# Attention in a fused fp32 kernel: new-key products once per pair of batches, five split heads instead of four, a weight split moved a stage ahead, tiles re-addressed

## The reference, cut to what matters

```python
x = x + einsum('bct,bcd->bdt', x, W0[ids0])                  # three small residual maps,
x = x + einsum('bsi,boi->bso', x, W1[ids0])                  # each batch with weights of its own
x = x + einsum('bct,bcd->bdt', x, W2[ids1]) + bias[ids1]
# attention over a paged cache: 64 batches, 32 new rows each, 32 query heads, 8 key heads, D = 128
q, k, v = x @ Wq.T, x @ Wk.T, x @ Wv.T                       # then norm and rotation of q and k
kc = k_cache[block_table]; vc = v_cache[block_table]         # 16 pages of 32 keys: 512 cached keys
scores = einsum('bqhd,bkhd->bhqk', q, concat([kc, k])) / sqrt(D)
scores = where(valid, scores, -1e30)                         # 512 cached + 32 new keys = 544
probs = softmax(scores)
x = x + (einsum('bhqk,bkhd->bqhd', probs, concat([vc, v])) @ Wo.T)
```

## Time and profile before

| | us |
|---|---|
| median of 3 runs | 2288.32 (2285.64 to 2289.05) |
| the profiled execution | 2286.66 |
| its span | 2284.8 |

### The profile page before, as it was taken

How to read it: one execution, slowest core, us unless ns; L and a number is a source line. 1 busy time by engine, 2 the same in 40 slices (tenths; PEclk the granted TensorE clock), 3 DMA queues, 4 the chain that set the end, 5 groups by cost and what they waited for, 6 DMA issues and landing times. The chain is left out here.

```text
span 2284.8 us, 52315 instructions
## 1 busy us (share of the span) xinstructions
PE 2231.2 (98%) x16384; PEld 1935.1 (85%) x16384; DVE 1675.9 (73%) x3504; ACT 1297.7 (57%) x2643; POOL 1137.8 (50%) x1218
## 2 busy tenths in 40 slices
PE   7998999999998999999999999999999998999999
PEld 6777777777776999999999999999999997888887
DVE  7860788888887888888888888888888886422221
ACT  6732888888886555555555555555555555311111
POOL 5200354544445777777777777777777773000000
PEclk9999999999998999999999999999999999999999
DMA  6643243444347888888888888888888885543442
GB/s 263 217 107 92 86 127 114 132 134 127 116 140 244 302 303 300 299 297 300 297 290 289 292 297 299 298 301 295 302 300 292 300 298 188 188 139 105 121 129 64
DMA packets 451816, 501.70 MB, mean 220 GB/s; under 512 B 95863, under 2 KB 390775, under 8 KB 443416
## 3 DMA queue, kind: packets, MB, share of 16 engines
q1 hardware_dynamic: 414872, 366.44, 49.3%
q0 software_dynamic: 36864, 134.23, 16.6%
HBM read 408.21 MB, written 92.34 MB: 219 GB/s over the span
## 5 line engine op out<-in xcount | busy, mean ns | idle before, releaser
L1192 POOL TENSOR_TENSOR att_probs<-att_probs,att_inverse 128x512 f32<-128x512 f32 x512 | 535.9, 1047 | 255.0 <-DVE att_inverse L1402 250.7
L1300 ACT ACTIVATE att_probs<-att_probs,att_low 128x544 f32<-128x544 f32 x512 | 383.7, 749 | 472.9 <-DVE att_low L1389 472.9
L1256 PE MATMUL att_o<-att_probs_t,att_values 128*128 128x128 f32 x4096 | 541.0, 275 | 2.1 <-DMA att_values<-L_cond_v_cache,att_v_rows_of 1.8
L1256 PEld LDWEIGHTS att_o<-att_probs_t,att_values 128*128 128x128 f32 x4096 | 497.6, 192 | 2.5 <-DMA att_values<-L_cond_v_cache,att_v_rows_of 2.0
L1389 DVE CUSTOM_DVE_ANT_0 att_probs<-att_score,att_mask,att_batch_cols 128x544 f32<-128x544 f32 x512 | 400.6, 782 | 129.2 <-PE att_score L1218 84.6
L1398 DVE COPY att_probs_t<-att_turn 128x512 f32<-128x512 f32 x512 | 351.0, 686 | 1.2 <-PE att_turn L1233 1.2
L1178 POOL DMA_INDIRECT att_values<-L_cond_v_cache,att_v_rows_of x256 | 270.8, 1058 | 82.5 <-POOL att_v_rows_of L1174 50.1
L1233 PE MATMUL att_turn<-ident,att_probs 128*128 128x128 f32 x2048 | 310.1, 274 | 0.8 <-POOL att_probs L1192 0.4
L1005 POOL TENSOR_TENSOR proj_q_out<-proj_by_cos,proj_by_sin 128x512 f32<-128x512 f32 x128 | 188.6, 1474 | 216.8 <-DVE proj_by_sin L931 216.8
L1233 PEld LDWEIGHTS att_turn<-ident,att_probs 128*128 128x128 f32 x2048 | 241.9, 141 | 36.2 <-issue 8.8
L862 PE MATMUL proj_proj<-x3t_hi,proj_w_hi 128*128 128x512 f32 x640 | 254.6, 398 | 6.7 <-DVE proj_w_lo L916 6.7
(11 more groups left out here) (156 smaller groups left out, 4101.1 us busy)
## 6 DMA issues: line engine op xcount, KB each, us to landing
keys_first<-L_cond_k_cache SPq DMA_DIRECT2D x512, 128.0 KB
att_keys_raw<-L_cond_k_cache SPq DMA_DIRECT2D x512, 128.0 KB
q_t<-proj_q_out SPq DMA_DIRECT2D x32, 1024.0 KB, 5.4
o_t<-att_heads_out SPq DMA_DIRECT2D x64, 512.0 KB, 6.6
out_o_raw<-o_t SPq DMA_DIRECT2D x31, 1024.0 KB, 5.3
queries_first<-q_t SPq DMA_DIRECT2D x32, 512.0 KB
att_queries_raw<-q_t SPq DMA_DIRECT2D x32, 512.0 KB
maps_even<-L_cond_weight SPq DMA_DIRECT2D x8, 1024.0 KB, 12.3
```

The costliest lines, as they stand in the source:

```text
L1192: nc.gpsimd.tensor_tensor(probs[:, k, 0:L], probs[:, k, 0:L], inverse[:, k:k + 1].to_broadcast([P, L]), ALU.mult).then_inc(probs_ready, 1)
L1256: last = nc.tensor.matmul(o_ps[:, at:at + P], values[j][:, t, h * D:(h + 1) * D], probs_t[m % 2][:, t * P:(t + 1) * P], start=(t == 0 and ...
L1300: nc.scalar.activation(probs[:, k, :], probs[:, k, :], ACT.Exp, bias=low[k][:, 0:1], scale=-1.0, accum_out=total[k][:, 0:1]).then_inc(exp_ ...
```

## The change

Five parts.

1. *One passage for a pair.* The products with the new values of both batches, 16 products, come once, in iteration 2 of the next pair. Each of the four banks of `o_ps` now holds the outputs of four heads of 128 columns, and the outputs of a pair go out in four copies, two in iteration 2 and two in iteration 3, into one tile. `new_probs_t` has four buffers. The outputs of both batches of the last pair are stored at the end.
2. *Five split heads.* NATIVE is 3, ACT_FROM 3, DVE_FROM 4: heads 3 to 7 are split. The parts grow from 384 and 512 to 480 and 640 elements, DVE writes the mask in head 3 and parts in heads 4 to 7, 0 and 1 (before: mask in head 4, parts in heads 5 to 7 and 0 to 2).
3. *The first head's weights* are split at the end of `stage_maps_values`, into buffers placed high. SP no longer waits there for the stores of the new values; POOL does so in the next stage. The wait for the stores of the new keys moves to the end of the projection.
4. *Addresses.* `keys_first`, `queries_first` and the first output head's `o0` lie in the high region. The built program places the value weights `wvt`, `o0`, `new_probs_t` and `heads_out` 32 bytes off a multiple of 64 before, and at multiples of 64 after.
5. POOL's first gather waits for the last weighing of the batch before (`weighed[1]`), where it waited for the passage.

```diff
-            w_hi[0] = a_.sb("w_hi0", [P, M, IC, P], F32R)          # now the high buffers w_first
+        a_.sb("to_64_bytes", [P, 8])
...
+            for m in range(1 + REP):                               # stage_maps_values, DVE, at the end
+                dve.wait_ge(w_hi_ready, m + 1)
+                nc_v.tensor_tensor(w_first_lo[:, m]..., w_nat[:, m, :], f32(w_first_hi[:, m])..., ALU.subtract).then_inc(w_ready, 1)
...
+            act.wait_ge(w_nat_loaded, 32)                          # stage_maps_values, ACT
+            for m in range(1 + REP):
+                copy(w_first_hi[:, m].rearrange("p c e -> p (c e)"), w_nat[:, m, :]).then_inc(w_hi_ready, 1)
...
-            for m in range(M):                                     # stage_projection, ACT and DVE
-                split_weights(0, 0, m, True)
...
-    NATIVE = 4
-    ACT_FROM, DVE_FROM = 4, 5
+    NATIVE = 3
+    ACT_FROM, DVE_FROM = 3, 4
...
-                            pool.wait_ge(o_done, i * N + j * HK)
+                            pool.wait_ge(weighed[1], i * HK + j * (HK // 2))
...
-                at = (h % GH) * BANK + (h // GH) * P
+                at = (m % GH) * BANK + (m // GH) * P
...
-                if h == HK - 1:
-                    pe.wait_ge(new_loaded[j], back * NLD + NLD)
-                    pe.wait_ge(new_kept, back * (N // GH) + (j + 1) * (HK // GH))
-                    for g in range(HK // GH):
+                if m == N - 1:
+                    for v in range(2):
+                        pe.wait_ge(new_loaded[v], back * NLD + NLD)
+                    pe.wait_ge(new_kept, back * (N // GH) + (N // GH))
+                    for g in range(N // GH):
...
-                    if h == 2 and (n >= HK or not first):
-                        keep_o(i, n - 3)
+                    if n in (2, 3) and not first:
+                        keep_o(i, range((n - 2) * 2, (n - 1) * 2))
```

More of the change, by code:

```diff
@@ L835, in _ @@
             heads(sp, head)
+            for rc in range(RC):
+                sp.wait_ge(k_stored[rc], 16 * HK)
         @block.tensor
@@ L874, in _, with split_weights @@
         def _(act):
-            def split_weights(h, u, m, first=False):
-                if m == 0 and not first:
+            def split_weights(h, u, m):
+                if m == 0:
                     act.wait_ge(w_loaded, h * 32)
@@ L975, in head @@
                         scale_k(h, SCALE_AT[t])
-            for m in range(M):
-                split_weights(0, 0, m)
             dve.wait_ge(first_pages_loaded, 16)
@@ L1008, in _ @@
             nc.gpsimd.memset(ones[:], 1.0).then_inc(ones_ready, 1)
+            for u in range(2):
+                pool.wait_ge(v_stored[u], 16 * GB * (G // 2))
             heads(pool, head)
@@ L1064, in stage_attention @@
         inverse = a_.sb("inverse", [P, RING])
-        new_probs_t = [a_.sb(f"new_probs_t{n}", [P, P]) for n in range(2)]
-        heads_out = [a_.sb(f"heads_out{v}", [P, HK, P]) for v in range(2)]
+        a_.sb("to_64_bytes", [P, 8])
+        new_probs_t = [a_.sb(f"new_probs_t{n}", [P, P]) for n in range(N // GH)]
+        heads_out = a_.sb("heads_out", [P, 2, HK, P])
+        a_.sb("foot", [P, 128])
         wot0_hi = a_.sb("wot0_hi", [P, REP, HID], F32R)
         wot0_lo = a_.sb("wot0_lo", [P, REP, HID], F32R)
-        o0_hi = a_.sb("o0_hi", [P, REP, CB, S], F32R)
-        o0_lo = a_.sb("o0_lo", [P, REP, CB, S], F32R)
+        o0_hi, o0_lo = o_first
         wo0_raw = w_nat[:, 0:REP, :]
@@ L1141, in _ @@
                 sp.wait_ge(q_stored[n], 16 * HK * (RC // 2))
-            for rc in range(RC):
-                sp.wait_ge(k_stored[rc], 16 * HK)
             sp.wait_ge(pages_ready, 1)
@@ L1308, in new_part, with keep_o @@
                 act.wait_ge(new_turned, back * (N // GH) + (g + 1))
-                if g >= HK // GH or not first:
-                    act.wait_ge(o_done, back * N + g // (HK // GH) * HK)
-                nc.scalar.activation(new_probs_t[g % 2][:], new_ps[:, 0:P], ACT.Copy).then_inc(new_kept, 1)
-            def keep_o(i, n):
-                m = n % N
-                back = i if n >= 0 else i - 1
-                j = m // HK
-                act.wait_ge(o_done, back * N + (j + 1) * HK)
-                act.wait_ge(o_stored[j], back * 16)
-                for r in (slice(0, GH // 2), slice(GH // 2, GH)):
-                    nc.scalar.activation(heads_out[j].rearrange("d (g r) n -> d r g n", r=GH)[:, r],
-                                         o_ps.rearrange("d (r k) -> d r k", r=GH)[:, r, 0:HK // GH * P].rearrange("d r (g n) -> d r g n", n=P),
+                if g == 0 and not first:
+                    act.wait_ge(o_done, i * N)
+                nc.scalar.activation(new_probs_t[g][:], new_ps[:, 0:P], ACT.Copy).then_inc(new_kept, 1)
+            def keep_o(pairs, banks):
+                act.wait_ge(o_done, pairs * N)
+                for v in range(2):
+                    act.wait_ge(o_stored[v], pairs * 16 - 16)
+                for r in banks:
+                    nc.scalar.activation(heads_out.rearrange("d v (g r) n -> d r (v g) n", r=GH)[:, r],
+                                         o_ps[:, r * BANK:(r + 1) * BANK].rearrange("d (g n) -> d g n", n=P),
                                          ACT.Copy).then_inc(o_ready, 1)
@@ L1357, in _ @@
             new_part(PAIRS, -1)
-            keep_o(PAIRS, -1)
+            keep_o(PAIRS, range(GH))
         @block.vector
```

84 lines of the change are left out of this document (47 added, 37 removed).

## The result

The changed kernel takes 2332.5 us (median, 2330.78 to 2334.57), the kernel before 2287.08 in the same comparison: a ratio of 1.0198 with a 95% interval of 1.0181 to 1.0216. The forecast was 2296 and the range ended at 2316. The direction was right and the size was not: 45 us instead of 10.

The account below looks back on a forecast made before the run. Prediction: PE's row and POOL's chain bound attention together (both 14.76 us). From 2286.66: POOL's chain +8.7, DVE +7.8, first pair +1, end +1.5, boundary -4.2, addresses -4.8, so +10.0; forecast 2296 us, range 2262 to 2316.

Parts of the forecast that it names:

- PE's own row: Attention: larger passage +0.45, lost passage -0.82, two more split heads -0.34; PE's row alone -0.71 us a pair.
- POOL's chain keeps the second batch: Heads 10 to 14: POOL's chain stays 14.76 us against PE's 13.77, so the pair comes to +0.28, +8.7 us over 31.
- DVE's longer parts: Attention: the part before masks 8 and 0 grows by 0.24 us; taken as 0.25 a pair, +7.8 us (0 to +22).
- The first rival: Attention: PE's row is all that counts, POOL's hold dissolves, DVE keeps up: -22 us there, 2258 in all; chance 0.25.
- The sentence of the prediction on the lock: DVE and POOL's shared port: the longer part starts only when POOL is done, the whole added 0.24 us behind the lock.
- DVE costs nothing: Attention: POOL holds, but late masks fall into PE's room: 2288.9 us, no change that can be told; chance 0.17.
- DVE costs all: Attention: DVE's longer parts cost +22 us instead of +7.8, 0.72 a pair: 2311 us; chance 0.15.
- remark on late keys: Attention loop: keys loaded later, behind the outputs' store one iteration more, would also end near 2311 us.
- Edges: Between maps and projection -4.2 us (-1.5 to -6.9); addresses in output and value products -4.8 (0 to -6).
- the 1 us hoped for from the clock: Projection's start: a shorter gap may spare part of the first 4 us at 1.2 GHz: -1 us (up to 2, or none).
- First pair and end of attention: First pair needs all six parts one head earlier: +1 us (0 to +2); end has four copies and larger passage: +1.5.

Follow-up runs that it names:

- e8: Changed kernel with four split heads and POOL's copy of the row numbers one head earlier: 2270.2 us, ratio 0.9925 to the kernel before.
- e16: Changed kernel with low parts of two pages (output not the reference's), next keys' loads ahead of the stores, row numbers copied one head earlier: 2271.6 us, ratio 0.9935.
- e6: Changed kernel with DVE writing low parts of only two pages of each keys part in the loop (output not the reference's): 2301.1 us, ratio 1.0063.
- e10: Changed kernel with next keys' loads ahead of the stores and row numbers copied one head earlier: 2311.7 us, ratio 1.0106.
- e3: Changed kernel's edges, addresses and five split heads, but a passage for each batch as in the kernel before: 2320.0 us, ratio 1.0150.
- e1: Changed kernel with SP's loads of the next pair's first keys ahead of the new values' loads and outputs' stores: 2334.2 us, ratio 1.0204.
- e12: Changed kernel with low parts of two pages (output not the reference's) and next keys' loads ahead of the stores: 2294.6 us, ratio 1.0035.
- e2: Changed kernel with four split heads as before, the one passage for a pair kept: 2297.9 us, ratio 1.0047.
- e14: Changed kernel with keys' loads ahead of the stores, row numbers copied one head earlier, gathers in heads 3, 4, 6, 7: 2328.2 us, ratio 1.0187.
- e7: Changed kernel with POOL's copy of the row numbers one head earlier: 2312.6 us, ratio 1.0107.
- e11: Changed kernel with keys' loads ahead of the stores, row numbers copied one head earlier, gathers in heads 3, 5, 7, 1: 2444.0 us, ratio 1.0681.

## Why the prediction was wrong, step by step

*PE's own row*: right where it could be seen. Iteration 2 was 3.44 (forecast 3.4 to 3.5), head 3 2.11, iteration 10 without its passage 2.17. With four split heads the terms give 37.11 + 0.45 - 0.82 = 36.74, and e8 has 36.72. The 36.40 of five split heads no run reached; e16 came to 36.72.

*POOL's chain keeps the second batch*: right in mechanism. With four split heads it held 14.97 against the 14.76 worked out, the passage cost 0.51 a pair where its terms without the split heads give 0.45, and moving the copy of the row numbers released it (e8). The first rival (PE's row alone, 2258) falls.

*DVE's longer parts, taken as 0.25 a pair with 0.72 as the upper end*: this is the step that failed. Shortening them gave back 1.04 (changed to e6) and 1.25 (e10 to e16). The five split heads, parts and PE's gain together, cost 1.01 on top of the passage and 1.29 without it, where the forecast's terms give 0.08 and -0.09. The pair's growth of 1.52 instead of 0.53 is most of the 36.5 us between forecast and result: (1.52 - 0.53) x 31 = 31. The working counted the longer part once, between the copy and the next mask. It treated the chain of POOL, 11.30 from the multiplication of head 2 to that of head 6, as a constant. But that chain held gathers of 1.12, and the 1.12 itself contained a wait for DVE's part, as the earlier trace rows show once a gather's end is held against a part's end. So 96 elements more made each such gather 0.10 longer, and head 4, which had no part before, now has one: some 0.4 in POOL's chain over the gathers in a row. e3, with a passage for each batch as before, shows the whole: the chain taken as 11.30 takes 12.07 in its median pair. That delayed the multiplications that the next parts wait for, and so the masks behind them, 8 and 0 among them. The sentence of the prediction on the lock spoke of the part that waits for POOL, and left out POOL that waits for the part.

The Trainium skill, page "SBUF — State Buffer", section "Who interferes with whom", has DVE instructions with two SBUF inputs contend with GpSimd instructions that read SBUF, with whoever issues first holding the other up. That agrees with the part that waits for the multiplication. The same section infers that such an instruction does not hold up descriptor generation, since that needs the write interface. Here every one of the 144 gathers issued during such a part ended 0.85 or 0.86 after it; for these gathers the measurement decides. An indirect gather also reads its row numbers, as `bass.IndirectOffsetOnAxis(ap=v_rows_of...)` in the kernel says; whether it waited with that or with its descriptors, no run here shows.

*Rivals.* "DVE costs nothing" (2288.9) falls with e6. "DVE costs all" (2311, chance 0.15) came nearest, 21 too low, and by its number only: its 0.72 a pair, too, had no POOL waiting for a part. Its remark on late keys was right in that they came late, and wrong in that they counted: with the keys ahead the pair changes by 0.17 at most (e1, e10, e12).

*Edges*: forecast -9.0 for boundary and addresses together, measured -6.4 (-4.1 to -8.7). The gap shrank by 3.2 as forecast, but the 1 us hoped for from the clock mostly did not come: 0.54 was granted for 3.6 us, where the earlier trace rows had 0.50 for 4. The maps stage ended 3.8 sooner instead of 1.9, how much of it by the addresses was not tried alone. The output's products gained 4 ns, not 5. The projection's extra 1.6 and the 0.7 behind it were in no term.

*First pair and end of attention*: both mis-sized. From the first scores to those of the second pair it took 45.05 instead of 42.07, 3.0 more where the forecast had 1 (0 to 2). The end cost more than its 1.5: PE stood 1.44 longer (3.70 for 2.26), the larger passage took 0.45 more, as in the loop, and then came the products at the lower clock, which the sum did not have.

*Left open*: why iteration 13 carries 2.8 and the part 1.92 in the changed kernel. That part (1258.38 to 1260.30) spans a whole gather and a multiplication; that it lets both go first is read from the rows and was not tried apart. Parts as slow as this one are not a matter of length: e2 has them with 384 elements (1.59) and e12 with 320 (1.53). e8, e10 and e16, with the row numbers early, have none.

## What to carry to other kernels

Before an engine's chain is taken as a constant, hold the ends of its instructions against what runs beside them on the other engines: a duration that is 0.12 above the shortest of its kind may be a wait that grows with the change. When work is made larger on an engine that alternates with another over something they share, its price is the whole alternation, counted as often as it repeats. A product moved away takes its room with it; look for who lived in that room, and move that engine's idle wait (here 0.8 for row numbers) elsewhere in the same step.

## What the runs showed of the hardware that was not expected

- An indirect gather issued while DVE writes a low part (two inputs in SBUF, the engines' on-chip memory) ends 0.85 to 0.86 after the part: 1.05 with 320 elements (e16), 1.12 with 384 (before), 1.22 with 480 (changed), 1.39 with 640 (e14). Where it meets no part it takes 0.98 to 1.01, and issued just ahead of a part it takes 0.98 to 0.99 and the part is not held up either (0.65 for 480 elements, 0.81 for 640, e14).
- Between POOL's copy of the row numbers and the gather that uses them lay 0.79 of idle time; with the copy one head earlier the gather followed the multiplication by 0.15 (e7).
- A gather that PE had to wait for landed 6.7 to 8.3 us after its issue in e11 (DMA share 0.80, PE waited up to 4.8) and 8.5 to 9.7 in e14 (0.86, up to 1.6).
- PE's clock fell to the lower level after it had stood 3.52 (0.54 granted over 222.8 to 226.4, PE busy 13.2 of the 13.2 us before the gap) and 3.70 (0.50 over 1971 to 1973). After the 2.26 at the end of attention in the kernel before, 1.00 was granted over 1922 to 1930.
